# First expert layer: the 177 inner rows of a tile split 96 + 81 instead of 128 + 49 for the down products

## What is computed

```python
# one routed expert e, for its tokens x (inner width 176)
h = silu(x @ w1[e].T + b1[e]) * (x @ w3[e].T + b3[e])
y = (h @ w2[e].T + b2[e]) * router_weight      # summed over the 6 experts of a token
# the shared expert: the same, with inner width 352, without a router weight
```

## Time and profile before

| what | value |
|---|---|
| median of 3 runs | 1092.68 us (1090.04 to 1092.77) |
| the profiled execution's own time | 1091.23 us |
| its span in the trace | 1089.4 us |
| TensorE busy, products | 916.6 us (84%), 4445 records |
| weight loads busy | 684.5 us (63%) |
| VectorE, ScalarE, GpSimd busy | 611.9, 338.6, 441.8 us |
| routed tiles of this layer | up products from 296.1 us to the last at 499.6 us of the span |
| mean granted TensorE clock | 0.914 of 2.4 GHz |

### The profile page before, as it was taken

The page is one execution under the profiler, slowest core; times in us unless marked ns, Lnnn a source line. Parts: engine busy times, 40 slices in busy tenths (PEclk is TensorE's granted clock), DMA queues, the critical chain, the costliest instruction groups (busy, mean ns, idle before and its releaser), DMA issues. The chain is left out here.

```text
span 1089.4 us, 14057 instructions
## 1 busy us (share of the span) xinstructions
PE 916.6 (84%) x4445; PEld 684.5 (63%) x4445; DVE 611.9 (56%) x1096; ACT 338.6 (31%) x601; POOL 441.8 (41%) x329
## 2 busy tenths in 40 slices
PE   2999999696699999999949959678358879899996
PEld 2887887694566666666749847557246745556564
DVE  5567767558533333442579888686688643222221
ACT  2343442412033333333424323343124331112121
POOL 2576675103267787673412210622182204122222
PEclk9899999796799999999979979699558989999999
DMA  6412110008735434654620010000100077222210
GB/s 242 160 42 83 41 41 1 1 2 326 269 72 84 81 69 79 143 73 115 194 77 1 1 35 1 1 1 1 43 1 1 1 287 296 88 39 44 37 32 11
DMA packets 38287, 84.77 MB, mean 78 GB/s; under 512 B 9693, under 2 KB 27485, under 8 KB 35582
## 3 DMA queue, kind: packets, MB, share of 16 engines
q1 hardware_dynamic: 22046, 64.63, 16.8%
q0 software_dynamic: 16176, 19.31, 10.8%
HBM read 71.23 MB, written 20.68 MB: 84 GB/s over the span
## 5 line engine op out<-in xcount | busy, mean ns | idle before, releaser
L2357 PE MATMUL ffn_GU<-ffn_W,ffn_XTB 128*128 x252 | 92.0, 488 | 1.4 <-DVE ffn_XTB L2266 1.4
L2250 DVE TENSOR_TENSOR ffn_GB<-ffn_GU,ffn_BIAS 128x352 f32<-128x352 f32 x63 | 33.1, 525 | 98.9 <-PE ffn_GU L2357 88.3
L1841 PE MATMUL ffn_GU<-ffn_W,ffn_XTB 128*128 x184 | 85.0, 605 | 0.2 <-issue 0.2
L2066 POOL DMA_INDIRECT kept_MARKED<-scratch_rows,kept_IDX x63 | 62.3, 989 | 56.0 <-DMA scratch_rows<-ffn_WEIGHT 31.4
L1661 POOL DMA_INDIRECT out_x<-ffn_YB,ffn_XB x23 | 35.8, 1558 | 119.2 <-DVE ffn_YB L1790 112.5
L2388 PE MATMUL ffn_DN<-ffn_W,ffn_HT 128*128 x252 | 77.1, 405 | 0.0
L2357 PEld LDWEIGHTS ffn_GU<-ffn_W,ffn_XTB 128*128 128x128 f32 x252 | 43.6, 191 | 34.4 <-issue 20.9
L1868 PE MATMUL ffn_DN<-ffn_W,ffn_HT 128*128 (+1 forms) x248 | 60.3, 387 | 4.5 <-issue 3.7
L2106 ACT ACTIVATE ffn_HG<-ffn_GB 128x176 f32<-128x176 f32 x63 | 22.0, 349 | 118.3 <-DVE ffn_GB L2250 81.6
L1779 DVE COPY ffn_XTB<-ffn_XP 128x256 f32<-128x256 f32 x23 | 9.8, 425 | 86.7 <-PE ffn_XP L1850 86.7
L1234 POOL TENSOR_TENSOR attn_E<-attn_E,attn_SM 128x1024 f32<-128x1024 f32 x16 | 30.5, 1904 | 63.0 <-DVE attn_SM L1268 63.0
(11 more groups left out here) (486 smaller groups left out, 2516.3 us busy)
## 6 DMA issues: line engine op xcount, KB each, us to landing
ffn_W<-in_f_w SPq DMA_DIRECT2D x9, 1536.0 KB, 6.6
ffn_W<-in_f_w SPq DMA_DIRECT2D x16, 608.0 KB, 17.6
attn_W<-in_L_pairs SPq DMA_DIRECT2D x8, 1088.0 KB, 5.0
scratch_rows<-in_rows_empty SPq DMA_DIRECT2D x1, 2967.0 KB, 14.6
ffn_XB<-scratch_rows SPq DMA_DIRECT2D x23, 129.0 KB, 2.1
ffn_BIAS<-in_f_bias SPq DMA_DIRECT2D x1, 2816.0 KB, 14.1
kept_STAGE<-in_f_w SPq DMA_DIRECT2D x1, 2048.0 KB, 8.5
kept_STAGE<-in_L_pairs SPq DMA_DIRECT2D x2, 768.0 KB, 6.8
```

The lines of the kernel that those rows point to most:

```text
L1841: last = pe.matmul(GU[:, m, :], x, weights(e, k * 2 * HID3 + m * HID3, HID3), start=k == 0, stop=k == KD - 1)
L2066: pool.indirect_dma_start(XB[:, i % NB, :], None, DR["rows0"][:, :], bass.IndirectOffsetOnAxis(ap=IDX[:, i:i + 1], axis=0)).then_inc(rows_ ...
L2250: dve.tensor_tensor(GB[:, n % 2, :], GU[:, n % 2, 0:2 * HID], BIAS[:, bass.ds(e * (2 * HID), 2 * HID)], ALU.add).then_inc(biased, 1)
L2357: last = pe.matmul(GU[:, n % 2, 0:2 * HID], XTB[:, i % 2, k * P:(k + 1) * P], flat[:, bass.ds(e * WIDTH0 + k * 2 * HID, 2 * HID)], start=k ...
```

## The change

The chunks of a routed tile become (0, 96) and (96, 81). As the start of a chunk no longer is a multiple of 128, the places in HP, HT and the weight block are counted by the chunk's index j; they are the same places as before (columns j x 128 of HP and HT, block j of the weights). The host packs w2's rows by the same pairs. The shared expert's chunks, all sizes of buffers and transfers, the copies and the order of the work remain.

```diff
+CUT = 96
...
                 def chunks(n):
-                    return [(c, min(P, hidden(n) + 1 - c)) for c in range(0, hidden(n) + 1, P)]
+
+                    return ((0, P), (P, P), (2 * P, 2 * HID + 1 - 2 * P)) if shared(n) else ((0, CUT), (CUT, HID + 1 - CUT))
...
-                            for c, rows in chunks(n):
-                                last = pe.transpose(HP[0:rows, c:c + P], h_rows(n)[:, c:c + rows], IDENT[:, :])
+                            for j, (c, rows) in enumerate(chunks(n)):
+                                last = pe.transpose(HP[0:rows, j * P:(j + 1) * P], h_rows(n)[:, c:c + rows], IDENT[:, :])
...
-                            for c, rows in parts:
+                            for j, (c, rows) in enumerate(parts):
                                 if shared(n):
-                                    w = WS[0:rows, 2 * UP0 + c // P * D:2 * UP0 + (c // P + 1) * D]
+                                    w = WS[0:rows, 2 * UP0 + j * D:2 * UP0 + (j + 1) * D]
                                 else:
-                                    w = flat[0:rows, bass.ds(e * WIDTH0 + UP0 + c // P * D, D)]
-                                last = pe.matmul(DN[:, n % 2, 0:D], HT[0:rows, n % 2, c:c + P], w, start=c == 0, stop=c == parts[-1][0])
+                                    w = flat[0:rows, bass.ds(e * WIDTH0 + UP0 + j * D, D)]
+                                last = pe.matmul(DN[:, n % 2, 0:D], HT[0:rows, n % 2, j * P:(j + 1) * P], w, start=j == 0, stop=j == len(parts) - 1)
...
-    def down(w, b, chunks):
-        rows = np.zeros((chunks * P, D), np.float32)
-        rows[:w.shape[1]], rows[w.shape[1]] = w.T, b
-        return rows.reshape(chunks, P, D).transpose(1, 0, 2).reshape(P, -1)
+    def down(w, b, parts):
+        rows = np.concatenate([w.T, b[None]])
+        placed = np.zeros((len(parts), P, D), np.float32)
+        for j, (c, n) in enumerate(parts):
+            placed[j, :n] = rows[c:c + n]
+        return placed.transpose(1, 0, 2).reshape(P, -1)
```

More of the change, by code:

```diff
@@ L2563, in up @@
         return np.concatenate([g.T.reshape(KD, P, -1), u.T.reshape(KD, P, -1)], 2).transpose(1, 0, 2).reshape(P, -1)
-    def down(w, b, chunks):
-        rows = np.zeros((chunks * P, D), np.float32)
-        rows[:w.shape[1]], rows[w.shape[1]] = w.T, b
-        return rows.reshape(chunks, P, D).transpose(1, 0, 2).reshape(P, -1)
-    each = np.stack([np.concatenate([up(a["w1"][e], a["w3"][e]), down(a["w2"][e], a["b2"][e], 2)], 1) for e in range(E0)])
-    shared = np.concatenate([up(a["ws1"], a["ws3"]), down(a["ws2"], a["bs2"], 3)], 1)
+    def down(w, b, parts):
[4 more added lines that the diff above has]
+        return placed.transpose(1, 0, 2).reshape(P, -1)
+    each = np.stack([np.concatenate([up(a["w1"][e], a["w3"][e]), down(a["w2"][e], a["b2"][e], ((0, CUT), (CUT, HID0 + 1 - CUT)))], 1) for e in range(E0)])
+    shared = np.concatenate([up(a["ws1"], a["ws3"]), down(a["ws2"], a["bs2"], ((0, P), (P, P), (2 * P, 2 * HID0 + 1 - 2 * P)))], 1)
     return each, shared
```

## The result

The changed kernel takes 1074.49 us (median of 4 runs, 1072.81 to 1078.52) beside 1091.36 of the kernel before (4 runs, 1085.45 to 1092.77): a ratio of 0.9863, interval 0.9823 to 0.9903. The forecast was 1082.5, the range 1079.5 to 1088.5. The direction held; the number came out lower than the range. The profiled execution took 1072.98 us against 1091.23 before, 18.2 us less, where the prediction had 10.0.

The account below looks back on a forecast made before the run. TensorE, paying 0.38 us a tile around the 49-row chunk, was taken as the bound, then a copy loop of 2.70 us. Gains of 8.1 + 1.45 + 0.47 = 10.0 us gave 1081.2 profiled, 1082.5 median; range 1079.5 to 1088.5.

Parts of the forecast that it names:

- The crossings: Routed down product: passing between 64 rows or fewer and more costs 0.19 us, twice a tile; without it TensorE needs 2.50.
- What is late next: Up product, bias add and XTB copy form a loop of 2.70 us, so a tile gains 0.18 and not 0.38.
- steady intervals: 45 of the 62 intervals between routed tiles, each gaining 0.18 us, 8.1 us together.
- behind a shared tile: Five intervals that also turn three shared chunks, falling from 2.99 to 2.70 us, 0.29 each.
- the five after those: Five intervals with the shared down product in them, which has no 49-row chunk: no gain.
- over a shared tile: Five intervals containing a shared tile, set by VectorE and ScalarE: no gain.
- tail: The last two down products, alone at the end of the stage, lose their crossings: 0.47 us gained.
- Costed at nothing: Transposes, ScalarE copies, weight transfers and GpSimd add no time; GpSimd's 11.8 us idle before the next stage covers its scatters.
- rival A: TensorE stays the bound in the routed tiles: period 2.50 us, 20 us gained, 1072.7; chance 0.07.
- B: The link from XTB copy to up load takes 0.36 us: period 2.81, 4.5 us gained, 1088.2; chance 0.11.
- D: TensorE drains at every change of row count, three times a down product: period 3.07, 9.8 us slower, 1102.5; chance 0.04.
- C: Loads of 49 and 128 rows take equally long, so the new split gains nothing: 1092.7; chance 0.07.

Follow-up runs that it names:

- one_wait: The changed kernel without TensorE's second wait before the up product, for the bias add of two items before; ratio 0.9909 to the kernel before.
- cut113: The changed kernel with routed chunks of 113 and 64 rows in place of 96 and 81; timed once, 1084.51 us.
- again_after: The changed kernel run again without an edit, on the first chip; median 1087.93 us, ratio 0.9905 to the kernel before.
- after_third: The changed kernel run once more without an edit, on the third chip; median 1086.14 us, ratio 0.9886 to the kernel before.
- pad49: The kernel before with its 128 + 49 split, but the second down matmul contracts over 128 rows, the extra ones zeros in the weights; ratio 0.9906.
- swap_after: The changed kernel with VectorE's copy of the next tile's XTB put ahead of the bias add; ratio 0.9917 to the kernel before.

## Why the prediction was right or wrong

**The crossings** were right. The earlier trace rows gave 0.19 us a crossing between 64 rows or fewer and more; the split at 113 keeps it, the one at 112 loses it, and TensorE alone needs 2.49 us a tile without it, where 2.50 was forecast.

**What is late next** was right, with its numbers: 1.60 + 0.85 + 0.24 forecast, 1.59 + 0.85 + 0.25 measured, and a period of 2.694. The choice of 0.24 over 0.36 for the link held. The reason given for it, that nothing else held the load there, was only part of it. A further wait instruction is 0.11 us of the 0.24, as one_wait shows.

**The intervals**, added up from the starts of the up products in the first profile:

| term | forecast | measured |
|---|---|---|
| steady intervals | 45 x 0.18 = 8.1 | 45 x 0.183 = 8.2 |
| behind a shared tile | 5 x 0.29 = 1.45 | 5 x 0.290 = 1.45 |
| the five after those | 0 | 5 x 0.104 = 0.5 |
| over a shared tile | 0 | 5 x 0.016 = 0.1 |
| first three, over their steady share | 0 | 1.0 |
| tail | 0.47 | 0.6 |
| the stage | 10.0 | 11.9 |

The term that I had put at nothing for the five intervals with the shared down product was mis-sized. They went from 3.025 to 2.921 us. Each begins with the up product of the second tile behind the shared one, and there the copy and the load are these:

```profile
327.95 0.41 DVE L2268 COPY ffn_XTB<-ffn_XP 128x256 f32<-128x256 f32 x1
...
328.50 0.31 PEld L2359 LDWEIGHTS ffn_GU<-ffn_W,ffn_XTB 128*128 128x128 f32 x2
```

Only one wait stands at this place, so the load comes 0.14 us behind the end of the copy (328.36 to 328.50), still under the last 81-row matmul, and ahead of its own product. The step of 0.40 to the second record that the earlier trace rows showed, and that I kept in the forecast, falls to 0.30 with a load pulled ahead: 0.10 a time.

The 1.0 of the first three intervals is no effect of the split. The first of them took 5.18 us before and 5.11 after, the second 3.79 and 2.92; cut113, with the crossings, has 5.06 and 2.92; the third, 2.87 and 2.59, is 2.77 there. In the two repeats the stage gave 9.5 and 10.0, and that this meets the forecast of 10.0 is partly luck. The first two intervals gained nothing there, as forecast (9.0 and 8.9 us together, where the two profiles of before have 9.0 and 8.9). The terms put at nothing gave about 0.7, and longer single intervals took 0.9 to 1.1 back: 3.35 and 3.18 us in again_after, 3.38 and 2.77 in after_third. Neither profile of before has such intervals, and what causes them wasn't settled.

**Costed at nothing.** Transposes and the ScalarE copies: pad49 agrees, with the old transposes and the new period. GpSimd: the conclusion held and the reason nearly failed. I said that 11.8 us of idle time cover scatters that start no earlier. Some 3.8 us of them are no cover, since GpSimd needs that long after its last scatter in any case, and the rest was used up but for 1.6 us. Had the loop been as fast as rival A has it, the 20 us of its sum would not have come: swap_after has A's period and its stage is 11.0 us shorter than before, in place of 20.

**The failed step** is the one sentence that sized everything outside the change: that "a shift of the later stages against the clock gate can move a microsecond either way". Between the two first profiles the stage of layers 1 and 2 and that of layer 3 differ by 2.6 and 5.1 us, all in one direction, 7.7 in place of 1. Only 1.7 of these are shown to go with the clock (66.96 us at 0.89, 65.31 at 0.91); the 5.1 go with the wait for something remote, which the prediction didn't have at all. The stage of the change alone would have given 1091.23 - 11.9 = 1079.3 for the profiled execution and 1092.68 - 11.9 = 1080.8 for the median, inside the range. With the repeats, the layer-3 stage takes 53.3 to 53.6 us or 58.8 to 61.7, with crossings in every tile (cut113, before) and without (the changed kernel, pad49) alike. The trace of before held a hint of it: a single wait of 7.9 us for something remote, in a stage that I never opened because the diff doesn't touch it. The range was built from the cases of one stage and had no width for what other stages do from one execution or chip to the next.

**The rivals.** B (link 0.36, period 2.81) and D (a drain at every change of row count, 3.07) fall by the period of 2.694 and by the steps of 0.21 and 0.22 around 96 and 81 rows. C (no change) falls by the ratios. Its premise was true: a load of 81 rows takes as long as one of 49, even a little longer (means of 190 and 184 ns); the time was never in the length of the load. A had the right bound for TensorE and the wrong one for the kernel.

**Open.** What the remote wait in layer 3 waits for, and why it stays away on one chip, wasn't settled. The 16.9 us of the first comparison therefore aren't shown to be the change's; 9.5 to 11.9 in its own stage are, and 10.4 and 12.5 by the two repeated ratios.

## What to carry to other kernels

When a contraction is cut into chunks, look at the distances between the starts of matmuls, not at their durations, and try to keep all chunks on the same side of 64 rows as the products around them; here zero rows up to 128 did as well as an even split. Before a gain is priced, work out the next two limits: here a copy one engine away took half of 0.38 us a tile, and behind it another engine's scatters took the other half once that was freed. Before a range is given, look through the stages that the change doesn't touch for single long waits, since another profile of the same kernel may not have them.

## What was not expected of the hardware

- A wait that had long been fulfilled cost 0.11 us when it stood as an instruction of its own between the last event and a weight load (0.25 us from copy to load with it, 0.14 without).
- GpSimd took no less than 3.66 to 3.83 us from the end of its last scatter to the first instruction of the next stage, in the three kernels in which it set the end. A DRAIN of 5.19 to 5.36 us on its sequencer, which starts before the record of the last scatter, ends just ahead of the new stage; it lasts 5.36 in before and the changed kernel too, where the others are later. What it waits for, the trace doesn't say.
- The border is sharp: 65 rows cost what 128 do (periods of 2.694 and 2.695 us), and 64 what 49 do (2.877 both). The Trainium skill (TensorEngine Tiling (Array Packing), When to Use Tiling) gives row tiling for a contraction of 64 or less; nothing here packs two such chunks side by side, and alone beside full-height products they only paid the 0.19 us a crossing.
- The same kernel has medians of 1089.06 and 1098.85 us on two chips, a difference as large as the gain that was to be measured. In the profiles of the other kernels, the layer-3 stage with its remote wait accounts for 5 to 8 us of such a difference, and a piece of layer 2's attention that lasts 65.3 or 67.0 us, at a mean granted clock of 0.91 or 0.89, for 1.7.
